# Gated cross-attention and expert block on one core: statistics one group further ahead, rows scaled by VectorE, and a new order inside the step

## The reference

```python
def layer_norm(x, gamma, beta):
    mu = jnp.mean(x, axis=-1, keepdims=True)
    var = jnp.mean(jnp.square(x - mu), axis=-1, keepdims=True)
    return (x - mu) * jax.lax.rsqrt(var + EPS) * gamma + beta
...
xn = layer_norm(x, g_x, b_x)          # x comes in through a plain layer norm already
cn = layer_norm(context, g_c, b_c)
q = (xn @ Wq).reshape(B, N, H, DH).transpose(0, 2, 1, 3)   # 16 heads of 64
k, v = ...                             # the same from cn
sim = jnp.einsum('bhid,bhjd->bhij', q, k) * scale
attn = jax.nn.softmax(sim, axis=-1)
out = jnp.einsum('bhij,bhjd->bhid', attn, v)
...
x = x + jnp.tanh(g_xattn[0]) * (out @ Wo)
n = _layernorm(x, axis=-1)
logits = n @ router_w                  # 14 experts, argmax, its softmax weight
x = x + jnp.tanh(g_ffn[0]) * weight * (gelu(n @ w1[e] + b1[e]) @ w2[e] + b2[e])
```

## Time and profile before

| | |
|---|---|
| median of 3 runs | 895.61 us (891.29 to 896.56) |
| profiled execution | 898.15 us, span 896.4 us |
| mean granted TensorE clock | 0.927 of 2.4 GHz |
| busy share of the span | PE 86%, PEld 78%, DVE 64%, ACT 57%, POOL 71% |

### The profile page before, as it was taken

How to read it: one execution, slowest core, us unless ns; L and a number is a source line. 1 busy time by engine, 2 the same in 40 slices (tenths; PEclk the granted TensorE clock), 3 DMA queues, 4 the chain that set the end, 5 groups by cost and what they waited for, 6 DMA issues and landing times. The chain is left out here.

```text
span 896.4 us, 34833 instructions
## 1 busy us (share of the span) xinstructions
PE 767.8 (86%) x12659; PEld 701.6 (78%) x12660; DVE 576.8 (64%) x1565; ACT 509.3 (57%) x986; POOL 632.4 (71%) x1230
## 2 busy tenths in 40 slices
PE   0899998999999999999999999999999974488882
PEld 0788888888888888888888888888888864488881
DVE  3256666777666767676767676767666762476772
ACT  2555666666665656666666565656556631365661
POOL 6666677777777777777777777777777655277774
PEclk9989999999999999999999999999999965598996
DMA  4651001110000000000000101010100000365540
GB/s 113 187 143 26 15 23 31 37 34 28 28 28 28 28 28 28 28 28 28 28 28 28 32 24 34 24 31 28 30 18 15 31 19 15 105 173 145 140 117 7
DMA packets 50526, 43.90 MB, mean 49 GB/s; under 512 B 14632, under 2 KB 46026, under 8 KB 50474
## 3 DMA queue, kind: packets, MB, share of 16 engines
q1 hardware_dynamic: 43898, 30.53, 12.8%
q0 software_dynamic: 5632, 12.67, 4.0%
q10 hardware_dynamic: 944, 0.01, 0.1%
HBM read 28.55 MB, written 15.68 MB: 49 GB/s over the span
## 5 line engine op out<-in xcount | busy, mean ns | idle before, releaser
L582 ACT ACTIVATE OT_h<-psO 128x1024 fp32r<-128x1024 f32 x64 | 65.7, 1026 | 127.2 <-PE psO L770 127.2
L474 POOL TENSOR_TENSOR probs<-probs,row_inv 128x1024 f32<-128x1024 f32 x64 | 121.8, 1904 | 7.8 <-DVE row_inv L1005 7.1
L985 DVE TENSOR_REDUCE row_max<-psS 128x16 f32<-128x1024 f32 x64 | 78.3, 1224 | 66.1 <-PE psS L748 66.1
L1000 DVE TENSOR_REDUCE row_sum<-probs 128x16 f32<-128x1024 f32 x64 | 77.7, 1215 | 66.6 <-ACT probs L595 66.6
L573 ACT ACTIVATE KT<-psJ 128x512 f32<-128x512 f32 x128 | 76.3, 596 | 54.8 <-PE psJ L691 49.3
L1013 DVE TENSOR_TENSOR OT_l<-psO,OT_h 128x1024 fp32r<-128x1024 f32 x64 | 78.1, 1221 | 26.6 <-ACT OT_h L582 26.5
L573 ACT ACTIVATE QT<-psJ 128x512 f32<-128x512 f32 x128 | 75.8, 594 | 20.9 <-PE psJ L691 18.0
L689 PE MATMUL psJ<-CT_h,Wk_h 96*128 96x256 f32 x256 | 85.4, 334 | 2.0 <-ACT QT L573 1.9
L770 PE MATMUL psO<-PTs,V 64*64 64x64 f32 x4096 | 85.6, 240 | 1.5 <-ACT PTs L589 0.8
L689 PE MATMUL psJ<-XT_h,Wq_h 128*128 128x256 f32 x256 | 81.6, 319 | 5.9 <-POOL CT_l L491 5.9
L573 ACT ACTIVATE V<-psJ 128x512 f32<-128x512 f32 x128 | 76.1, 595 | 15.0 <-PE psJ L691 11.8
(11 more groups left out here) (172 smaller groups left out, 2302.9 us busy)
## 6 DMA issues: line engine op xcount, KB each, us to landing
V<-rows_by_expert SPq DMA_DIRECT2D x40, 129.0 KB
QT<-rows_by_expert SPq DMA_DIRECT2D x40, 129.0 KB, 2.3
x_in<-in_x_dram SPq DMA_DIRECT2D x32, 128.0 KB, 2.2
x_res<-in_x_dram SPq DMA_DIRECT2D x32, 128.0 KB, 2.4
c_in<-in_ctx_dram SPq DMA_DIRECT2D x32, 96.0 KB, 2.3
rows_by_expert<-pad_row SPq DMA_DIRECT2D x1, 1806.0 KB, 12.7
w_sb<-in_L_ffn_w_dram SPq DMA_DIRECT2D x1, 1792.0 KB, 8.1
rows_by_expert<-rows,place_i POOLq DMA_INDIRECT x64, 2.7
```

Of the source, the lines that this page charges most:

```text
L474: pool.tensor_tensor(pr, pr, row_inv[:, p.k % 2, :].unsqueeze(2).to_broadcast([P, 16, SEQ]), ALU.mult).then_inc(s_norm, 1)
L985: dve.tensor_reduce(row_max[:, :], psS[:, :].rearrange("p (n k) -> p n k", k=SEQ), AX.X, ALU.max).then_inc(s_max, 1)
L1000: dve.tensor_reduce(row_sum[:, :], pr, AX.X, ALU.add).then_inc(s_sum, 1)
```

## The change

The statistics of incoming rows are taken three groups ahead instead of two, and `roots` works on them one group earlier, so that `norm_in` uses the roots of the step before. `norm_in` and `norm_x2` move from GpSimd to VectorE, with the same operations. In the lists of the step, several pieces change places. TensorE: in the odd step `value_sums` and job 9 stand ahead of `prep`; in the even step the first `probs_T` stands behind `post_a`, and the router behind job 3. ScalarE: in the odd step `expo` ahead of job 10, and the second `probs_out` ahead of `attn_out`. VectorE: in the odd step `norm_x2` and `prep` stand between the maximum and its subtraction; in the even step `norm_in` follows `stats_in`, `means_in` follows the subtraction, and `sums` comes ahead of `values_low`. The start is rewritten to match: it takes the statistics of group 0, then of 1 and 2, with the low parts of the weights (`low`) between them. The semaphore `s_scaled` goes.

```diff
@@ roots (GpSimd)
-                g_in, g_x2 = p.group(-2), p.group(2)
+                g_in, g_x2 = p.group(-3), p.group(2)
...
-                n = NEWT * (p.g + 2)
+                n = NEWT * (p.g + 3)
                 if g_in is not None:
-                    pool.wait_ge(s_agg, 4 * (p.g + 3))
+                    pool.wait_ge(s_agg, 4 * (p.g + 4))
...
-                if not (p.fixed and p.g < -1):
-                    if not (p.fixed and p.g + 1 >= GROUPS):
-                        pool.wait_ge(s_z, 4 * (p.g + 2))
-                if not (p.fixed and not 0 <= p.g - 3 < GROUPS):
+                if not (p.fixed and p.g + 2 < 0):
+                    pool.wait_ge(s_z, 4 * (p.g + 3) if not p.fixed else 4 * min(p.g + 3, GROUPS))
+                if not (p.fixed and p.g - 3 < 0):
                     pool.wait_ge(s_n2, 2 * (p.g - 2))
@@ GpSimd's step and start: norm_in and norm_x2 go
                     roots(p)
-                    norm_in(p)
                     normalise(p)
-                    norm_x2(p)
-
+
+            roots(Plan(-2, 2))
+            split_in(Plan(-1, 0))
             roots(Plan(-1, 0))
-            norm_in(Plan(-1, 0))
-            split_in(Plan(-1, 0))
+            split_in(Plan(-1, 2))
             roots(Plan(-1, 2))
-            norm_in(Plan(-1, 2))
-
-            split_in(Plan(-1, 2))
@@ ScalarE's odd step
                     norm_T(p)
+                    expo(p)
                     job(p, 10)
-                    expo(p)
                     probs_out(p, 0)
+                    probs_out(p, 1)
                     attn_out(p)
-                    probs_out(p, 1)
                     job(p, 11)
@@ TensorE's odd step
                     job(p, 8)
+                    job(p, 9)
+                    value_sums(p)
                     prep(p)
-                    value_sums(p)
-                    job(p, 9)
                     probs_T(p, 0)
@@ TensorE's even step
                     post_a(p)
+                    probs_T(p, 0)
                     job(p, 2)
+                    job(p, 3)
                     router(p)
-                    job(p, 3)
-                    probs_T(p, 0)
                     job(p, 4)
@@ VectorE
+            def norm_in(p):
+
+                if p.group(-2) is None:
+                    return
+                par = p.par()
+                dve.wait_ge(s_newton, NEWT * (p.g + 3))
+                if not (p.fixed and p.g < -1):
+
+                    dve.wait_ge(s_prep, p.g + 2)
+                for t in range(2):
+                    dve.tensor_scalar(zx[:, t, :], x_in[:, par, t, :], rstd[:, t:t + 1], shift[:, t:t + 1],
+                                      ALU.mult, ALU.subtract).then_inc(s_z, 1)
+                for t in range(2):
+                    dve.tensor_scalar(zc[:, t, :], c_in[:, par, t, :], rstd[:, 2 + t:3 + t], shift[:, 2 + t:3 + t],
+                                      ALU.mult, ALU.subtract).then_inc(s_z, 1)
+
+            def norm_x2(p):
+
+                if p.group(2) is None:
+                    return
+                par = p.par()
+                dve.wait_ge(s_newton, NEWT * (p.g + 4))
+                for t in range(2):
+                    dve.tensor_scalar(rows[:, par, t, D:2 * D], rows[:, par, t, 0:D], rstd[:, 4 + t:5 + t],
+                                      shift[:, 4 + t:5 + t], ALU.mult, ALU.subtract).then_inc(s_n2, 1)
...
                 if p.odd:
                     scores_max(p)
+                    norm_x2(p)
+                    prep(p)
                     scores_sub(p)
-                    prep(p)
                     weight(p)
                     values_low(p)
                     sums(p)
                 else:
                     stats_in(p)
-                    means_in(p)
+                    norm_in(p)
                     scores_max(p)
                     scores_sub(p)
+                    means_in(p)
                     residual(p)
                     means_x2(p)
                     route(p)
+                    sums(p)
                     values_low(p)
-                    sums(p)
                     places(p)
@@ VectorE's start
+            def low(i):
+                lo, hi, raw = lows[i]
+                dve.wait_ge(s_wh, i + 1)
+                dve.tensor_tensor(lo, raw, hi, ALU.subtract).then_inc(s_wl, 1)
+
+            g0, g1, g2 = Plan(-2, 2), Plan(-1, 0), Plan(-1, 2)
+            stats_in(g0)
+            means_in(g0)
+            stats_in(g1)
+            low(0)
+            norm_in(g1)
+            means_in(g1)
+            dve.wait_ge(s_small, N_SMALL)
+            prep(g1)
+            low(1)
+            stats_in(g2)
+            norm_in(g2)
+            means_in(g2)
+            low(2)
+            prep(g2)
+            low(3)
```

More of the change, by code:

```diff
@@ L188, in gated_block_kernel @@
         s_stat2, s_agg2 = sem("s_stat2"), sem("s_agg2")
-        s_newton, s_scaled = sem("s_newton"), sem("s_scaled")
+        s_newton = sem("s_newton")
         s_z = sem("s_z")
@@ L437, in roots @@
                 pool.tensor_tensor(shift[:, :], mv[:, :, 0], rstd[:, :], ALU.mult).then_inc(s_newton, 1)
[L439 to L467, removed]
             def normalise(p):
@@ L944, in stats_in @@
             def stats_in(p):
-                if p.group(-2) is None:
+                if p.group(-3) is None:
                     return
[L948 to L952, removed]
+                par = p.par(-3)
+                dve.wait_ge(s_in[par], 32 * p.uses(-3))
+                if not (p.fixed and p.g < -2):
+                    dve.wait_ge(s_agg, 4 * (p.g + 3))
                 for t in range(2):
@@ L958, in means_in @@
             def means_in(p):
-                if p.group(-2) is None:
+                if p.group(-3) is None:
                     return
-                if not (p.fixed and p.g < -1):
-                    dve.wait_ge(s_newton, NEWT * (p.g + 2))
-                dve.wait_ge(s_stat, 4 * (p.g + 3))
+                if not (p.fixed and p.g < -2):
+                    dve.wait_ge(s_newton, NEWT * (p.g + 3))
+                dve.wait_ge(s_stat, 4 * (p.g + 4))
                 dve.sem_inc(s_aggr, 1)
@@ L1122, in _ @@
                     (Wo_l[:, :, :].rearrange("p m d -> p (m d)"), Wo_h[:, :, :].rearrange("p m d -> p (m d)"), raw_o))
[L1123 to L1129, removed]
-                    dve.tensor_tensor(lo, raw, hi, ALU.subtract).then_inc(s_wl, 1)
-                if g == -2:
-                    dve.wait_ge(s_small, N_SMALL)
-                prep(q)
+            def low(i):
[18 more added lines that the diff above has]
+            low(3)
             dve.wait_ge(s_tanh, 1)
```

## The result

The changed kernel takes 916.52 us (915.3 to 917.91), the kernel before 894.33 in the same session: a ratio of 1.0251, 95% interval 1.0214 to 1.0288. The forecast was 835, range 824 to 868, with a chance of 0.05 for slower. The profiled execution took 915.3 us, its span is 913.5.

The account below looks back on a forecast made before the run. TensorE was taken as the bound, interrupted once a group by a 1.5 us wait. Loop 53.7, group ahead 1.0, start 3.7 and end 3.3 made 61.7 us less: 835 us, range 824 to 868.

Parts of the forecast that it names:

- The chain of the wait: TensorE's 1.5 us wait per group for GpSimd's scaled rows goes with statistics a group further ahead: 27 x 1.5 = 40 us.
- What is late next: In the loop, waits of 0 to 0.1 at the probability transposes, 0.1 to 0.2 at the values' low part; period 20.2 us.
- one job less of lead: The router on TensorE has one job less of lead over the residual; nothing was put on it.
- VectorE's added work: Six scalings a group at 0.3 us each, some 0.2 apart: 1.2 us; VectorE busy 16.5 to 18 of 20.2.
- The bound of 0.45: Upper limit in us for one moved scaling on VectorE: six a group add at most 2.7 us.
- rival (a): Partly blocked: the last VectorE scaling stands behind GpSimd's `normalise`; period 21.3 us, 864 us, 880 with clock dips; chance 0.15.
- a margin of 0.3 to 0.5 us: VectorE's last scaling starts at 7.5 to 7.7 us in the group, ahead of GpSimd's `normalise` at 7.97.
- The argument "against": Against blocked scalings: the margin, and indirect DMA issues hardly lengthening beside VectorE's copies (0.280/0.294, one of 0.552).
- Rival (c): Slower: all four VectorE scalings start after `normalise` if sums end 1.1 us late; job 4 waits 2.7; 920 us; chance 0.05.
- The rule: VectorE and GpSimd share one port pair, held for a whole instruction; moved scalings could be held up by `normalise` or delay it.
- The clock: In the loop, TensorE's clock stays at 1.00 once it is fed, saving 12 x 1.4 = 17 us of dips.
- Start: Ahead of the first TensorE job, scaling on VectorE and less stretched GpSimd operations save 3.7 us; first job near 18 us.

Follow-up runs that it names:

- experiment 1: The changed kernel with `norm_in` moved behind `scores_sub` in VectorE's even step; 834.64 us, ratio 0.9357 to the kernel before.
- experiment 3: The changed kernel with `norm_in` first in VectorE's even step and `stats_in` behind `scores_sub`; 888.6 us, ratio 0.9917 to the kernel before.
- experiment 4: The changed kernel with `norm_in`'s scalings written as one operation with two SBUF inputs, same place; 924.54 us, ratio 1.0358 to the kernel before.
- experiment 7: The changed kernel with GpSimd's odd-step `normalise` made to wait for the following step's four input scalings; ratio 0.9581 to the kernel before.
- experiment 5: The changed kernel with all scalings, those of the start too, back on GpSimd; 842.25 us, ratio 0.9408 to the kernel before.
- experiment 6: The kernel of experiment 1 with `weight` also moved ahead of `prep` in the odd step; 828.45 us, ratio 0.9266 to the kernel before.
- experiment 8: The kernel before with only the input statistics one group further ahead, scalings on GpSimd, old order; ratio 0.9432 to the kernel before.
- experiment 2: The kernel before with only the new order of TensorE, ScalarE and VectorE; 875.88 us, ratio 0.9804.

## Why the prediction was wrong

**The chain of the wait.** Right. L665 waits no more, and with the scalings unhindered the kernel takes 834.6 us (experiment 1), where 835 was forecast for the change. The terms, measured there: period 20.30 (20.2 forecast), loop start 4.9 earlier (3.7 + 1.0 forecast), what lies behind the loop 9.1 shorter (3.3 forecast, up to 4.5). Of these, 5.1 are in the drain, and 3.9 in the expert stage (from its first copy `KT<-w_sb` to the end, 125.4 us before and 121.5 in experiment 1), which the prediction called untouched. No run shows why.

**What is late next.** The path through split, send and `normalise` was right to 0.01 us, the start of the scalings to 0.3 in one kind of group and 0.7 in the other. The router got nothing ("one job less of lead"); in the changed kernel it is the first place where the lateness comes out, ahead of job 4, which was named.

**VectorE's added work.** 0.34 and 0.32 against 0.3, starting 0.25 apart: right, where nothing stops them. VectorE is then busy 17.4 of 20.4 us (experiment 1), within the 16.5 to 18 of the prediction. The bound of 0.45 didn't hold the 2.76 of a stopped one, which makes it 19.2.

**The step that failed is the margin in rival (a)**: "a margin of 0.3 to 0.5 us", reckoned from the start of the last scaling to the row of `normalise` at 7.97. Two things were wrong with it. First, the race isn't decided at that row: a `normalise` that is ready behind an issue holds VectorE's scaling off well ahead of its row. The first scaling of the group at 459.44 starts 467.41 - 466.60 = 0.81 us ahead of it and passes; the longest one in the changed kernel starts 0.75 ahead (119.20, the row at 119.95) and is held for 2.76. In the changed kernel and in experiment 3, behind a scatter issue, every scaling that starts 0.80 us or more ahead passes and every one that starts 0.77 or less ahead is held. (With the other form, in experiment 4, one passes at 0.73; those held start 0.57 or less ahead.) So the limit is at 7.97 - 0.8 = 7.2: the first scaling (7.16) just gets through and the second (7.4) doesn't. By the prediction's own starts, the last at 7.5 to 7.7, the margin was some -0.4, not +0.4. Second, the starts came later than worked out, by 0.3 us, and by 0.7 once in each trip of the loop. So even by the row the last scaling (about 0.75 us behind the first) had a margin of 0.1 in one kind of group and was 0.4 late in the other. Experiment 3 takes 0.7 us off the starts and parts the two: its later kind starts at 6.9 to 7.6, all ahead of the row, and is still held at 7.4.

The argument "against" read the earlier trace rows as showing that indirect DMA issues hardly lengthen. The row gives the copies of VectorE, which hardly lengthen. Experiment 7 shows that an issue by itself is indeed nearly harmless, but it hides a `normalise` that is already waiting behind it.

**Rival (c)** had the outcome, 920 against 916.5, and its mechanism (all of the scalings' followers behind `normalise`, job 4 late, dips), but asked for sums 1.1 us later than worked out as its point. They were 0.3 later (`stats_in` starts 6.4 after L665, 6.1 was worked out), and it happened all the same, because of that 0.8 us: in twelve of 25 groups all four scalings end behind `normalise`. That the number comes within 4 us of 920 is partly luck: at full clock a group takes 21.9 us, not 22.7, and the dips are in 19 of 27 windows, not in half. Its chance of 0.05 and the 0.15 of (a) rested on the same margin; with the price of losing so high and the margin a few tenths, the chances should have been nearer to even.

**The rule.** The Trainium skill (SBUF — State Buffer, "Who interferes with whom") says that whoever issues first gets the shared pair for the whole instruction. The trace agrees on the whole instruction, with 2.57 us for a scaling of 0.34 beside 1.91 of `normalise`. On the order it doesn't agree, if one goes by the rows: the held scaling's row starts first, by up to 0.77 us. It also says that an operation with two inputs from SBUF contends with a GpSimd operation that reads it; in experiment 4 such a one is stopped as long as the other form.

**The clock.** "With TensorE fed I expect 1.00 everywhere" held in the loops of experiments 1, 5, 6, 7 and 8. A shorter stand doesn't always dip less. In the changed kernel 0.8 or 1.0 us at the router and 0.3 at job 4 go with 19 dips in 27 windows (of eleven windows with the 0.8 seven dip, of 13 with 1.0 or more twelve), the 1.1 and 0.3 of experiment 2 with one, and the 1.5 of before with twelve. What else decides stays open.

**Start.** The first job comes at 20.05, where 18 was forecast and 21.99 was before. The trace of the changed kernel shows what stands there:

```profile
9.70 0.20 POOL L436 TENSOR_TENSOR shift<-mv,rstd 128x6 f32<-128x6 f32 x1
...
10.98 0.49 DVE L919 BATCH_NORM_STATS2 bn<-x_in 128x6 f32<-128x128 f32 x2 [5.79 <-DMA c_in<-in_ctx_dram]
...
12.83 0.60 DVE L944 TENSOR_SCALAR zx<-x_in,rstd,shift 128x128 f32<-128x128 f32 x2
```

The roots are there at 9.9, but the scalings stand in VectorE's order behind `stats_in` of the second group, which waits for its input until 10.98, and behind the first `low`. So 2.9 us pass between the two; the forecast has them follow at once. No run moves these pieces.

## What to carry to other kernels

When work moves to VectorE, look up in the trace of before what GpSimd runs at that time, and not at its row alone: an operation that is released and queued behind a DMA issue already keeps VectorE out, so a margin under a microsecond ahead of its row is none, and the loss (here 2.3 us of VectorE's time a group, and the clock) has to be priced at even odds. Look at more than one group too: here every second one starts VectorE's step 0.4 us later. The remedy can be as cheap as two places in VectorE's order. And run each part of a change by itself: here one part held nearly all of the gain, and the place of another all of the loss.

## What the runs showed of the hardware

- GpSimd's queue behind a scatter issue of 0.98 us: a VectorE scaling that starts 0.44 us into the issue, with the GpSimd operation behind it released, ends only with that operation, after 2.57 us; with that operation not yet released, one that starts 0.43 in takes 0.34.
- That hold reaches 0.77 us ahead of the row of `normalise`, and not 0.80. It isn't a fixed time ahead of a row: in the even step, where GpSimd's small operations and no issue stand ahead of a released `normalise`, `place` starts 0.47 or 0.65 us ahead in experiment 1 and takes 0.18.
- VectorE, SBUF to SBUF, f32, two column operands: 0.34 us for 128 columns, 0.32 for 96, one every 0.25.
- A small operation isn't safe either: `place` (28 columns, 0.18 us) is stopped for up to 1.93 us when it starts just behind the start of `normalise` (experiment 7).
- One program can show both outcomes in turn, group by group (20.29 and 23.89 us), and its runs still agree within 1%.
